# Keys and values of the second cross attention as products of high and low parts, in one core's perceiver program, with batches dealt 2, 2, 31, 13, 12, 4 in place of 2, 2, 30, 11, 15, 4

## What is computed

```
x = x + xattn0(LN(x), ctx, mask)     # cross attention, ctx is 64 x 257 x 256
x = x + delta(LN(x))                 # short convolutions, delta rule in chunks of 32, FIR filters, gates
x = x + moe0(LN(x))                  # 8 experts, top 2, gathered rows
x = x + xattn1(LN(x), ctx)           # the second cross attention: 16 heads of 16
x = x + selfattn(LN(x))              # rotary, grouped keys
x = x + moe1(LN(x))                  # 16 experts, shared part
```

```
k = _split_heads(K @ Wk.T + bk)      # K = V = ctx
v = _split_heads(V @ Wv.T + bv)
```

## Time and profile before

| | us |
|---|---|
| median of 3 runs | 1621.93 (1618.51 to 1623.67) |
| span of the profiled execution | 1609.7 |
| median less the span | 12.2 |
| PE busy of the span | 1490.3 (93%) |
| DVE, ACT, POOL busy | 1100.2, 813.9, 583.5 |

### The profile page before, as it was taken

One profiled execution on the slowest core, in us unless ns is written; L12 is line 12 of the kernel. 1 busy time (PEld: TensorE's weight loads), 2 busy tenths in 40 slices (PEclk: granted clock), 3 DMA queues, 4 the chain that ended last, 5 costly groups with the idle time before them and its releaser, 6 DMA issues. The chain is left out here.

```text
span 1609.7 us, 38473 instructions
## 1 busy us (share of the span) xinstructions
PE 1490.3 (93%) x15176; PEld 1144.1 (71%) x15176; DVE 1100.2 (68%) x2412; ACT 813.9 (51%) x1848; POOL 583.5 (36%) x487
## 2 busy tenths in 40 slices
PE   5998999989988999999999989999899788999998
PEld 3454468544456579999998646666688686799997
DVE  4588869974047456666563558888599676767887
ACT  1233742121143336666654449999277422766663
POOL 2440310000011026777645346787288452121210
PEclk9899999999999999999999989999999999999999
DMA  9993048532024357676658317664000010010001
GB/s 327 316 354 97 1 156 219 133 73 46 1 80 137 110 209 278 217 274 239 237 181 222 96 50 246 204 209 129 27 1 1 18 30 15 1 34 21 27 1 53
DMA packets 114074, 203.99 MB, mean 127 GB/s; under 512 B 38073, under 2 KB 74361, under 8 KB 108009
## 3 DMA queue, kind: packets, MB, share of 16 engines
q1 hardware_dynamic: 91481, 107.72, 22.5%
q0 software_dynamic: 10032, 57.55, 10.3%
q10 hardware_dynamic: 12384, 36.27, 6.8%
HBM read 161.67 MB, written 39.83 MB: 125 GB/s over the span
## 5 line engine op out<-in xcount | busy, mean ns | idle before, releaser
L2387 POOL TENSOR_TENSOR a_pr<-a_pr,a_inv 128x1028 f32<-128x1028 f32 x64 | 122.2, 1909 | 63.6 <-DVE a_inv L2515 63.6
L386 PE MATMUL ps<-kv_ctx,kv_w 128*128 128x257 f32 x464 | 121.5, 397 | 8.5 <-ACT kv_kv L410 3.0
L390 PE MATMUL ps<-kv_w,kv_ctx 128*128 128x256 f32 x464 | 117.2, 397 | 8.3 <-ACT kv_kv L410 8.3
L2479 ACT ACTIVATE a_pr<-ps,a_neg 128x257 f32<-128x257 f32 x256 | 119.0, 473 | 2.7 <-DVE a_neg L2531 2.3
L2531 DVE TENSOR_REDUCE a_neg<-ps 128x2 f32<-128x514 f32 x128 | 87.9, 688 | 41.9 <-PE ps L2404 40.9
L1631 POOL TENSOR_TENSOR b0m_pm<-b_dr,b_gates 128x256 f32<-128x256 f32 x16 | 13.2, 829 | 279.3 <-SPq L1595 250.4
L390 PEld LDWEIGHTS ps<-kv_w,kv_ctx 128*128 128x128 f32 x464 | 89.4, 199 | 28.8 <-ACT kv_kv L410 14.6
L386 PEld LDWEIGHTS ps<-kv_ctx,kv_w 128*128 128x128 f32 x464 | 86.7, 197 | 26.8 <-issue 13.6
L3389 DVE SCALAR_TENSOR_TENSOR x<-ps,g_gate,x 128x256 f32<-128x256 f32 x256 | 105.1, 475 | 0.0
L972 DVE SCALAR_TENSOR_TENSOR b_F<-b_F,b_fir 128x992 f32<-128x992 f32 (+29 forms) x128 | 96.7, 792 | 0.0
L2415 PE MATMUL ps<-ident,a_pr 128*128 128x128 f32 x512 | 81.2, 281 | 16.3 <-ACT a_prT L2486 10.9
(11 more groups left out here) (447 smaller groups left out, 4433.1 us busy)
## 6 DMA issues: line engine op xcount, KB each, us to landing
late_kv<-kv SPq DMA_DIRECT2D x52, 513.0 KB, 4.4
kv<-kv_kv ACTq DMA_DIRECT2D x46, 513.0 KB, 5.4
a_ctxT<-in_ctxT SPq DMA_DIRECT2D x32, 514.0 KB, 9.7
a_ctxR<-in_ctx SPq DMA_DIRECT2D x32, 512.0 KB
kv_ctx<-in_ctxT ACTq DMA_DIRECT2D x34, 257.0 KB, 3.4
kv_ctx<-in_ctxT SPq DMA_DIRECT2D x24, 257.0 KB, 4.6
outs<-f_yo SPq DMA_DIRECT2D x16, 256.0 KB, 4.5
a_vB<-vlast SPq DMA_DIRECT2D x32, 128.0 KB
```

The lines of the kernel that those rows point to most:

```text
L386: done = e.matmul(out[:, 0:NK], self.w[:, 0, c, cols(part)], ctx[:, c, :], start=(c == 0), stop=(c == DC - 1))
L390: done = e.matmul(out[:, cols(t, D)], ctx[:, c, cols(t)], self.w[:, 1, c, :], start=(c == 0), stop=(c == DC - 1))
L2387: e.tensor_tensor(pr[:, b % RP, :, :], pr[:, b % RP, :, :], inv[:, b % 2, :].unsqueeze(2).to_broadcast([P, HG, NK]), ALU.mult).then_inc(*p ...
L2479: e.activation(pr[:, b % RP, r, :], K.ps[:, bank(b, r), 0:NK], ACT.Exp, bias=neg[:, b % 2, r:r + 1], accum_out=tot[:, b % 2, r:r + 1]).the ...
```

## The change

Every K and V matmul in f32 becomes a `product3` of fp32r operands: three records where there were two, the keys now 258 columns wide (`WIDTH` is 257, with a cleared column behind it). For this the weights are split on GpSimd once (`split_weights`, at the end of cross attention 0, from a buffer `wkv` whose loads now stand on SP ahead of the keys of tile 14). Each batch's context is rounded by ACT (`round_to`, 128 x 514, up to two batches ahead, behind the eviction of the values and ahead of the store), and the low part is subtracted by GpSimd (`low`, 128 x 2 x 257), or by DVE for the 12 batches of the tail. A slot of the context is reloaded once the low part is taken (it was: once PE is done), and ACT issues the reload behind the store. The split parts lie in a ring of two batches (three in the router).

To make room for the split parts, three buffers move: `sq` into a free part of `F`, `braw` into `xnb`, and `f1` (the 2 MB of `W_fuse1`) into `qk`, which the grams read. So its load waits for the last gram (`t_G.at(NT)`) and stands on SP behind all the loads of `A` and `M`. PE's wait for it stands where it stood: right behind the grams, ahead of the parts. There are now 17 parts in place of 14 at that place, 9 in place of 3 behind the router's named tables (so they are the 26th to 34th of its 39), and 36 in place of 45 in the tail.

```diff
-AHEAD = (2, 2, 30, 11, 15, 4)
+AHEAD = (2, 2, 31, 13, 12, 4)
...
+    def round_to(self, e, last):
+
+        for b in range(self.rounded, last):
+            raw, (high, _) = self.ctx[self.slot_of[b]], self.split_of(b)
+            e.wait_ge(*self.ld_c[self.slot_of[b]].at(16 * (len(self.before(b)) + 1)))
+            if self.split_before(b) is not None:
+                e.wait_ge(*self.mm.at(3 * self.split_before(b) + 3))
+            e.activation(high[:, :, 0:NK], raw, ACT.Copy).then_inc(*self.high.up())
+            self.rounded = b + 1
+
+    def low(self, e, last):
+
+        for b in range(self.lowered, last):
+            raw, (high, low) = self.ctx[self.slot_of[b]], self.split_of(b)
+            e.wait_ge(*self.high.at(b + 1))
+            e.tensor_tensor(low[:, :, 0:NK], raw, high[:, :, 0:NK].bitcast(F32), ALU.subtract).then_inc(
+                *(self.v_low if b in self.low_by_dve else self.p_low).up())
+            self.lowered = b + 1
...
             if part == 0:
-                e.wait_ge(*self.ld_c[s].at(16 * (len(self.before(b)) + 1)))
+                e.wait_ge(*self.low_done(b))
...
                 for c in range(DC):
-                    done = e.matmul(out[:, 0:NK], self.w[:, 0, c, cols(part)], ctx[:, c, :], start=(c == 0), stop=(c == DC - 1))
+                    done = product3(e, out[:, 0:self.WIDTH], [w[:, 0, c, cols(part)] for w in self.w], [x[:, c, :] for x in ctx],
+                                    c == 0, c == DC - 1)
...
             if part == 2:
-                if b + self.SLOTS < self.BY_SYNC:
-                    self.load(e, b + self.SLOTS)
+                self.round_to(e, min([b + 1 + self.LEAD, self.last // 3] + [x for x, _ in self.parts if x > b]))
                 e.wait_ge(*self.ev.at(j + 1))
                 place.store(e, self.K.kv[b])
+                for x in range(self.loaded, min(self.rounded + self.SLOTS, b + self.LEAD + self.SLOTS, self.BY_SYNC)):
+                    self.load(e, x)
...
                 for t in range(1, NT):
+                    if t == NT - 2:
+                        A.load_weights(e, wkv)
                     keys(t)
...
-        f1 = sb("f1", [P, 8, 512])
+        f1 = qk[:, 2:4, :].rearrange("p c (k n) -> p (c k) n", n=512)
...
-                e.dma_start(f1[:, :, :], features(K.ins["L0_attn_W_fuse1"])).then_inc(*ld_f.up(16))
...
+                e.wait_ge(*t_G.at(NT))
+                e.dma_start(f1, features(K.ins["L0_attn_W_fuse1"])).then_inc(*ld_f.up(16))
...
                 e.wait_ge(*ld_f.at(16))
-                ahead.pe(e, 14)
+                ahead.pe(e, 17)
                 fuse_most(0)
...
+                ahead.low(e, ahead.lowered + 1)
                 for t in range(NT):
...
+                    if t % 2:
+                        ahead.low(e, ahead.lowered + 1)
...
+                A.clear(e, A.TAIL - AHEAD[3])
+                A.low(e, A.TAIL - 2)
                 e.wait_ge(*v_row.at(3))
                 gather1(0)
                 gather1(1)
+                A.low(e, A.TAIL - 1)
                 e.wait_ge(*st_r.at(16 * NT))
                 gather2(0)
+                A.low(e, A.TAIL)
                 e.wait_ge(*v_token.at(1))
                 gather_rows(0)
...
                     if j == 0:
                         turned(1)
+                        e.wait_ge(*A.mm.at(3 * A.TAIL))
                     low2(j)
...
+                    A.low(e, min(A.TAIL + A.LEAD + t + 1, A.QUERIES))
                     K.norms["a1"].tile(e, t, v_x.at(2 * t + 2))
```

More of the change, by code:

```diff
@@ new lines, in clear @@
+    def clear(self, e, first):
+        for at in [x for x in self.parts if x[0] == first][0][1]:
+            for part in at:
+                e.memset(part[:, :, NK:self.WIDTH].bitcast(F32), 0.0)
+    def round_to(self, e, last):
[6 more added lines that the diff above has]
+            self.rounded = b + 1
@@ L516, in cross_attention_0 @@
     KS, GT = 4, 4
+    A = K.keys
+    K.split = Layer(K, "kvs", "right")
+    A.split_into(0, split_places(K.split.sb("parts", [P, A.LEAD, 2, DC, A.WIDTH], F32R)))
     K.front = DeltaWeights(K)
-    A = K.keys
     A.host(AHEAD[0], (6, 7), A.own)
@@ L1424, in _ @@
                 logits_back()
+            @block.gpsimd
+            def _(e):
+                ahead.low(e, ahead.formed // 3 + ahead.LEAD)
             @block.scalar
@@ L1539, in _ @@
                 ahead.pe(e, 4)
+            @block.gpsimd
+            def _(e):
+                ahead.low(e, ahead.formed // 3 + 1)
             @block.scalar
```

100 lines of the change are left out of this document (76 added, 24 removed).

## The result

The changed kernel takes 1673.35 us (median of 4 runs, 1671.09 to 1677.04) against 1621.93: a ratio of 1.0328 with a 95% interval of 1.0301 to 1.0355. The forecast was 1657.0 with a range of 1631 to 1681. The direction and the range held; the slowdown is 51 us where 35 were forecast. The two waits that the forecast named are in the trace. Most of what was missing lies in the router and in delta_mix.

The account below looks back on a forecast made before the run. Bound by stage: loads in cross attention 0, DVE in the grams, PE in later stretches, PE and gathers in the tail. Terms 4.0+20.1+0+14-2.5-0.5 = +35.1 on 1609.7, plus 12.2 outside the span: 1657.0 us, range 1631 to 1681.

Parts of the forecast that it names:

- The two waits that the forecast named: PE waiting about 24 us for W_fuse1 right behind the grams, and turn(0) waiting 5 us or more for gathered rows.
- What a part costs: Keys and values on PE: a batch gets 0.69 us cheaper, 44 us for 64 if all were on the path.
- Cross attention 0 and b0a: Start of the kernel: earlier weight loads, the wait for the first low part and ACT's rounding cost +4.0 us.
- delta_solve: Largest term, +20.1 us: W_fuse1 lands at 301, PE idle until then; ends +12 and +31.
- Gates and delta_mix: Nine cheaper batches against a GpSimd subtraction joining each pair of tiles: 0 us, ends -3 and +4.
- Router: Rows' gather held up on GpSimd by low parts, the 13th needing PE's 33rd part: +14 us, ends +9 and +17.
- Tail: 12 batches in place of 15, gathers and combination not shortened: -2.5 us, gain 0 to 4.
- its last term: Queries: a later start of 2 us and cheaper parts, -0.5 us.
- What lies outside the span: Whole kernel: 12.2 us outside the span, as before, added to a span of 1644.8 us.
- The router is not held up and subtractions are free: Rival: router costs about 0 to 3 us and delta_solve 17, giving 1640 us; chance 0.18.
- Contention in full: Rival: low parts hold up DVE and W_fuse1 lands at 311; +10 in delta_solve, +5 in mix and router, 1674 us; chance 0.16.
- PE's time is the path: Rival: cheaper PE batches shorten the gram loop, delta_mix and tail (18.7 us there), -11 in all, 1611 us; chance 0.08.

Follow-up runs that it names:

- the run with two columns: Changed kernel with each low part's subtraction cut to 2 columns and the high part given to product3 in place of the low: 1651.58 us, ratio 1.0223.
- the runs with the gathers first: Changed kernel with the router's first gathers ahead of the low parts of batches 10 to 13: 1664.85 us; with those low parts on DVE as well: 1668.86 us.
- the run with the gathers first: Changed kernel with the low parts of the router's batches 10 to 13 put behind the first gathers on GpSimd: 1664.85 us, ratio 1.0307.
- the two runs on contention: Kernel before with 11 GpSimd instructions of 128 x 512 added from delta_solve's start: as subtractions 1625.13 us, ratio 1.0040; as clearings 1619.66 us, ratio 1.0015.
- the deal alone: Kernel before, f32 matmuls kept, with only the new distribution of parts (17 for 14 in delta_solve, 9 for 3 behind the named tables): 1627.42 us, ratio 0.9999.
- the three mends: Changed kernel with W_fuse1's load and wait moved, router gathers first with four low parts on DVE, Wk and Wv loaded later: 1653.39 us, ratio 1.0228; again 1647.93.

## Why the prediction was right or wrong

The sign, the range and the two waits came as forecast. By the traces (61.1 for 35.1) the forecast is 26 us short: 8.5 in the router, 7.6 in gates and delta_mix, 4.8 from turn(0) to the queries, 4.0 in the rest that the change leaves as it is, and 1.1 in delta_solve. By the medians it is 16 short, so some of the 26 is the one fast execution of before.

1. **What a part costs: right.** The stretch of 17 parts measured 22.86 us (22.4), about 1.5 of it from the lower clock behind the wait, which the forecast did not have there, and the product with 8 parts 31.6 (31.7). PE's busy time fell by 14.7 us, not by 44: product3 records overlap more, so their busy time says less than their starts.
2. **Cross attention 0 and b0a: right in sum (+4.2 for +4.0), wrong in one cause.** 1.5 of it was put down to the weights' 512 KB; moving them later gained nothing, and cutting the subtractions gained 2 to 4.
3. **delta_solve: right, with some luck.** W_fuse1 landed at 306.2, which is 301 + 4.2 of shift + 1.0. PE's wait was 20.25 where 24.4 were worked out, since the grams ended 4.7 us later than forecast by the stage's start: contention took there what the wait then lacked. That is the luck: the 3 us which the forecast says it counted for contention here stand in none of its terms, and cost nothing because SP's queue, not the grams, set the landing. The move alone, on the kernel before, costs 19 us. Where I wrote that nothing hides the wait since it is ahead of the filler: moving it behind the filler hid only 6.5 us of 20.
4. **Gates and delta_mix: the term that failed in kind.** I wrote that nine cheaper batches and nine subtractions balance, -3 to +4; it was +7.6, outside. I took a subtraction at 1.04 us, its price alone; beside DVE's two-input steps it took 1.70, and the pair went from 5.83 to 6.39 (the run with two columns shows 5.53). The eight pairs make 3.6 us of the 7.6; the rest is the stage's start, where the first low parts stand ahead of the first products (1.5), and its end (2.5). With subtractions of two columns delta_mix is 7.8 us shorter, 76.3, within 1 us of the 77 of before. So the subtractions make all of it, and of the 6.2 us that the cheaper batches were to give hardly any is there even without them: DVE sets the pace.
5. **Router: right mechanism, undersized (+22.5 for +14, end +17).** The 33rd part did hold the rows' gather: 13.5 us from the tables' end to its issue, where 11.8 were worked out. Missed was what the 11th low part holds: the gathers of 3 MB of weights, issued at 637.51 and no longer 10 us ahead of the rows' but 7, and then in the way of them. I had kept "the same 7.4 from issue to turn(0)"; it was 12.2. (In the runs with the gathers first the 10.2 to 10.8 to turn(0) are not the rows' time: PE waits for nothing there, its parts fill them.) That is 4.8 us; "in the way" is read from traces, not from a run that moves those gathers alone. With the weights 6.6 to 6.8 us ahead of the rows the first rows take 12.2 to 14.3 in five traces (where PE waits for them, to its product); in the run with the gathers first, 8.4 ahead, they landed in 7.1, and on the kernel before, 9.6 to 9.9 ahead, in 7.4 to 9.5. 1.7 more were the named tables, 4.7 late and not 3, and 1.7 the eight parts. For these two the trace shows the cause: PE ran them at the lower clock until 636.3. The tables' own product took 2.4 us more than before, and the parts up to 636.3 about 2 more than the later ones; the forecast had put the clock at +1 in all.
6. **Tail: -2.5 forecast, about 0 measured.** From the last expert's product to the end of the normalisation it took 52.4 for 52.6. The +2.3 of the table is 0.9 between turn(0) and hidden(1) and the queries' later start, about 2, which the forecast had counted in its last term. That gathers set the pace was right; but DVE's low part of the third batch stands behind its first combination, which waits for a gather, and PE waited 7.8 us for it and then ran at the lower clock until 923.0:

```profile
917.24 0.58 PE L126 MATMUL ps<-f_w2H,kv_wH 128*128 128x258 f32 x1 [7.83 <-DVE f_w2H L422]
```

7. **What lies outside the span: wrong, without effect on the forecast.** I took the 12.2 us between span and median as lying outside the span. Only 1.9 do; the rest was a profiled execution faster than most. It stands on both sides of the forecast's difference and drops out. But 61 us of the traces stand against 51 of the medians, and in which stages the trace of before was fast can't be told, so the terms above should be read with some 2 to 5 us of doubt for the long stages.
8. **The rivals.** "The router is not held up and subtractions are free" fell with the wait of 14.1 and with the two runs on contention. "Contention in full" (1674, though its terms add up to 1672) gives the measured time, but by chance: it put 10 us more on delta_solve, which took 1.1 more than forecast. "PE's time is the path" is refuted by the time, and its largest term, the 18.7 us of the tail, by the deal alone, whose tail got no shorter.
9. **What is not accounted for.** The subtractions cost 17 to 22 us and the three mends give 16 to 20, together 33 to 42 of 51. They were not run together, so they may overlap. No run takes out the rounding on ACT or the lower clock.

## What to carry to other kernels

Before cheaper matmuls are bought with a rounding and a subtraction for each operand, ask which engine is busy beside the subtraction: on GpSimd, beside DVE steps that take both inputs from SBUF, each one costs both engines. Here the subtractions, their length and what they cost DVE together, took 17 to 22 us; in a pair of tiles of delta_mix they cost 0.86 us where the cheaper products gave 0.30. When the new operands need room, look at which load loses its own buffer: a 2 MB load that waits for the last reader and stands last on its queue cost 19 us by itself, and moving the wait for it behind other work gave back only a third, since the load then came later. On a queue in order, put gathers whose inputs come early ahead of work that waits for another engine. And read the granted clock beside every new wait: the work behind such a wait ran at half the clock for another 6 to 12 us here.

## What the runs showed of the hardware

A GpSimd subtraction of 128 x 512 takes 1.04 to 1.28 us alone and 2.03 to 2.11 beside DVE's filter steps, and 11 of them make these steps 7.2 us longer. A clearing of the same size takes 0.52 in either case and costs DVE nothing. A subtraction of two columns takes 0.70 instead of 0.19 when it starts just behind a DVE addition of 0.69 us with both inputs in SBUF: it ends with the addition, which is no longer for it.

The granted clock fell to half in and behind PE's long waits (20.25 us in delta_solve, 7.8 in the tail), and records of products behind them came 0.21 us apart instead of 0.12. In the deal alone a tail with less work for PE ended later, with the clock at half from 897.1 to 914.2.

One kernel's time varied more than the forecast had allowed for: the kernel before ran from 1608 to 1640 us over the chips used, and the stage of the experts, with the same instructions, took from 234.6 to 242.0 us in fourteen traces. The traces show where the difference lies. PE's idle time in the stage goes from 2.6 to 7.8 us, and in eight of the traces the clock was low for one stretch of 3.4 us. Less the idle time and half of that stretch, all fourteen lie between 232.1 and 233.1 us (counted to the end of the last product). The trace puts nearly all of that idle time to no engine or DMA, so its cause was not found.
